# Making the first head pair's q and k by token blocks inside the first normalization, with most of V between the first pair's attention steps

## The reference

```
h = layernorm(x)
q, k, v = h @ Wq + bq, h @ Wk + bk, h @ Wv + bv      # 16 heads of 64
q, k = rope(q), rope(k)
attended = softmax(causal(q k^T / 8)) v
x = x + attended @ Wo + bo
g = layernorm(x)
xq = fp4(g);  wq = fp4(weights)                      # blocks of 16, max/6 scale, E2M1 grid
x = x + fp4(silu(xq @ wg^T) * (xq @ wu^T)) @ wd^T    # hidden width 2816
```

## Time and profile before

| what | us |
|---|---|
| median of 3 runs | 1466.71 |
| lowest, highest | 1452.48, 1481.68 |
| the profiled execution | 1454.53 |
| its longest span (core 3) | 1453.0 |
| spans of all cores | 1430.1 to 1453.0 |
| busy on core 3: PE, DVE, ACT | 1128.6, 1053.6, 785.0 |

### The profile page before, as it was taken

One profiled execution on the slowest core, in us unless ns is written; L12 is line 12 of the kernel. 1 busy time (PEld: TensorE's weight loads), 2 busy tenths in 40 slices (PEclk: granted clock), 3 DMA queues, 4 the chain that ended last, 5 costly groups with the idle time before them and its releaser, 6 DMA issues.

```text
span 1453.0 us, 18420 instructions; the slowest of 8 cores (1430.1 to 1453.0 us)
## 1 busy us (share of the span) xinstructions
PE 1128.6 (78%) x6112; PEld 466.1 (32%) x6112; DVE 1053.6 (73%) x1189; ACT 785.0 (54%) x1116; POOL 98.3 (7%) x195
## 2 busy tenths in 40 slices
PE   1996878778878787871595627999999999999997
PEld 0332222222222222220131213444444444444443
DVE  3453799978898979882731237888888888888885
ACT  2553868767777778882641344444444444444443
POOL 1001001010101010120111100000000000000000
PEclk9998999988889999995797958999999999999999
DMA  9624658595859695679587530000000000000000
GB/s 209 161 78 97 130 125 182 137 160 121 195 126 180 121 174 133 156 154 264 108 214 270 161 112 1 30 30 30 30 30 30 29 30 29 30 30 30 15 15 30
DMA packets 110636, 152.01 MB, mean 105 GB/s; under 512 B 76288, under 2 KB 77776, under 8 KB 107728
## 3 DMA queue, kind: packets, MB, share of 16 engines
q1 hardware_dynamic: 96112, 103.31, 29.2%
q0 software_dynamic: 14432, 47.54, 14.3%
HBM read 102.38 MB, written 32.11 MB: 93 GB/s over the span
## 4 chain that ended last, share of the span: by engine, by line
DVE 30%; PE 28%; DMA 19%; issue 14%; ACT 6%; POOL 2%; SPq 1%; DVEq 1%; ACTq 0%; POOLq 0%
PE ps L1048 13%; DMA rb<-rscr 5%; DMA xscr<-x_t 5%; PE ps L513 4%; PE ps L1088 4%; DVE qs_bm L275 3%; DVE sm_bm L275 3%; DVE qy L305 3%; DVE qx L300 3%; PE ps L571 3%; DMA rscr<-rn 2%; DMA sw<-qk 2%; DMA bqks<-bqk 2%; DMA qx<-wd 2%; DVE h_u L1075 2%
## 5 line engine op out<-in xcount | busy, mean ns | idle before, releaser
L705 ACT ACTIVATE PT<-ps,nb 128x1024 bf16<-128x1024 f32 (+1 forms) x320 | 301.0, 986 | 24.5 <-PE ps L693 13.3
L686 PE MATMUL ps<-qk 64*128 64x512 bf16 (+3 forms) x640 | 125.1, 383 | 145.8 <-ACT PT L705 124.9
L1048 PE MATMUL ps<-wgT,xqT 128*128 128x512 bf16 (+1 forms) x768 | 193.0, 400 | 5.3 <-ACT xqT L1022 5.3
L293 ACT ACTIVATE sm_nsh<-sm_bmc 128x64 f32<-128x64 f32 (+1 forms) x64 | 16.2, 253 | 314.7 <-DVE h_u L290 287.4
L1048 PE MATMUL ps<-wuT,xqT 128*128 128x512 bf16 (+1 forms) x768 | 175.2, 372 | 0.0
L1088 PE MATMUL ps<-wdT,hqT 128*128 128x512 bf16 x704 | 161.3, 382 | 5.8 <-ACT hqT L1022 5.8
L571 PE MATMUL ps<-xlT,wqk 128*128 128x512 bf16 x512 | 134.5, 413 | 20.2 <-ACT PT L705 17.3
L725 PE MATMUL ps<-PT,V 128*64 128x512 bf16 (+3 forms) x640 | 128.1, 397 | 0.4
L686 PEld LDWEIGHTS ps<-qk 64*128 64x128 bf16 x640 | 35.6, 94 | 284.3 <-issue 283.5
L725 PE MATMUL ps<-PT,ones 128*64 128x512 bf16 (+3 forms) x640 | 121.5, 377 | 0.0
L1048 PEld LDWEIGHTS ps<-wgT,xqT 128*128 128x128 bf16 x768 | 79.5, 106 | 90.2 <-issue 32.2
(11 more groups left out here) (97 smaller groups left out, 1556.4 us busy)
## 6 DMA issues: line engine op xcount, KB each, us to landing
qx<-wg SPq DMA_DIRECT2D x22, 512.0 KB, 4.5
qx<-wu SPq DMA_DIRECT2D x22, 512.0 KB, 4.3
x_a<-x SPq DMA_DIRECT2D x16, 512.0 KB, 6.8
sw<-qk POOLq DMA_DIRECT2D x64, 128.0 KB, 3.7
qx<-wd SPq DMA_DIRECT2D x16, 512.0 KB, 4.4
x_t<-x POOLq DMA_DIRECT2D x16, 512.0 KB, 4.8
out<-x_t SPq DMA_DIRECT2D x16, 512.0 KB, 2.6
rb<-rscr POOLq DMA_DIRECT2D x14, 512.0 KB, 9.2
```

The source lines that it names most:

```text
L686: ins = te.matmul(PS[k].ap()[:, 512 * h + o:512 * h + 512], q[r, 1, kc * 128:(kc + 1) * 128], q[r, 0, qb * 512 + o:(qb + 1) * 512], start= ...
L705: exp_a[n] = act((lambda c: c.activation(PT[j].ap()[:, :, o:512], sc[:, :, o:512], AFT.Exp, bias=nb12.ap(), scale=0.125)), [(sPE, pp)] + ( ...
L1048: ins = te.matmul(bank[:, 0:cn], xqT[t % 2].ap()[:, kc, :], w.ap()[:, n0:n1, kc, :], start=(kc == 0), stop=(kc == KC - 1))
```

## The change

Block b of the normalization no longer makes V. After each second block, 512 tokens are complete: q and k of pair 0 for them are made at once (`qk_half(0, which, b // 2)`), swapped (`swap_first`), and rotated in the next block (`rope_first`, three DVE operations over q and k of 512 tokens, with the tables broadcast). Three pieces of weight jobs go into a block instead of two; the twelve pieces that stood around the old q and k of pair 0 are gone, and four stand around V of tiles 0 to 3, which comes after the loop. V of tiles 4 to 15 is made and copied out at steps 0, 2, 3, 4, 6, 8, ... 20 of pair 0. Pair 0 takes 1.6/8.6 of the remaining weight jobs. `norm_recip` moves from step 5 to 8 and `norm_mult` from 14 to 24 (19 in the last pair); the last pair's own move too. The first loads are ordered anew: the q and k bias by SP, V's weights on POOL behind the first q and k weights and the rotation tables.

```
@@ loads
-        for j in range(4):
-            wv_ld = dma("gpsimd", sWV, ...)
-        dma("gpsimd", sCST, bvs[:], bv_h)
-        dma("gpsimd", sCST, bos[:], bo_h)
-        cst = dma("gpsimd", sCST, bqk[:], bqk_h)
+        bqk_ld = dma("sync", sBQ, bqk[:], bqk_h)
...
         load_wqk(0)
         dma("gpsimd", sTAB, cosb[:], cos_h)
         tab = dma("gpsimd", sTAB, sinb[:], sin_h)
+        dma("gpsimd", sCST, bvs[:], bv_h)
+        cst = dma("gpsimd", sCST, bos[:], bo_h)
+        for j in range(4):
+            wv_ld = dma("gpsimd", sWV, ...)
         load_wqk(1)
@@ qk_half
-            pp = pe(f, [(sWQ[p % 2], wq_ld[p]), (sACT, evac_done),
+            pp = pe(f, [(sWQ[p % 2], wq_ld[p]), (sACT, a_evac[4 * tb + 3]),
@@ new
+        def swap_first(tb):
+            sl = slice(tb * 512, (tb + 1) * 512)
+            for g in range(4):
+                o, i = 32 * g, 32 * (g ^ 1)
+                sw_d[0, tb] = dma("gpsimd", sSZ[tb], sw.ap()[o:o + 32, :, sl],
+                                  raw[0].ap()[i:i + 32, :, sl],
+                                  [(sACT, qk_a[0, 1])])
+
+        def rope_first(tb):
+            sl = slice(tb * 512, (tb + 1) * 512)
+            q = raw[0].ap()[:, :, sl]
+            s = sw.ap()[:, :, sl]
+
+            def bc(table):
+                return table.ap()[:, sl].unsqueeze(1).broadcast_to(
+                    [128, 2, 512])
+            dve((lambda v: v.tensor_tensor(q, q, bc(cosb), Alu.mult)),
+                [(sSZ[tb], sw_d[0, tb]), (sTAB, tab)])
+            v2 = dve((lambda v: v.tensor_tensor(s, s, bc(sinb), Alu.mult)),
+                     [])
+            rope_tb[tb] = dve((lambda v: v.tensor_tensor(
+                q, q, s, Alu.add)), [(sDVE, v2)])
@@ loop over b
             vn = ln1_negm(b, a)
-            pump(1)
+            pump(2)
             for t in (t0, t0 + 1):
                 ln1_apply(t, vn)
                 if t + 4 < NT:
                     load_xa(t + 4)
-            if b >= 1:
-                v_evac(t0 - 2)
-                v_evac(t0 - 1)
             for t in (t0, t0 + 1):
                 ln1_transpose(t)
                 ln1_evac(t)
-            for t in (t0, t0 + 1):
-                v_proj(t)
-        v_evac(NT - 2)
-        v_evac(NT - 1)
+            if b % 2 == 1:
+                for which in range(2):
+                    qk_half(0, which, b // 2)
+                swap_first(b // 2)
+            elif b:
+                rope_first(b // 2 - 1)
+        for t in range(4):
+            v_proj(t)
+            if t >= 1:
+                v_evac(t - 1)
+            pump(1)
+        v_evac(3)
+        rope_first(3)
@@ scores
-            pp = pe(f, [(sDVE, rope_v[p, 0]), (sDVE, rope_v[p, 1]),
-                        (sACT, sc_free[k])])
+            ws = ([(sDVE, rope_tb[qb])] if p == 0 else
+                  [(sDVE, rope_v[p, 0]), (sDVE, rope_v[p, 1])])
+            pp = pe(f, ws + [(sACT, sc_free[k])])
@@ whole_pair
-            share = (QTOT - q0) / (NP - p)
+            share = (QTOT - q0) * (1.6 / 8.6 if p == 0 else 1 / (NP - p))
...
+                if p == 0 and s in V_AT:
+                    v_proj(V_AT[s])
+                    v_evac(V_AT[s])
...
-                if prev_tok and s == 5:
+                if prev_tok and s == 8:
                     norm_recip(prev_tok[0])
-                if prev_tok and s == 14:
+                if prev_tok and s == (24 if p + 1 < NP else 19):
                     norm_mult(prev_tok.pop(0))
@@ last_pair
-            for qb, at_r, at_m in ((0, 16, 20), (1, 22, 28), (2, 34, 38)):
+            for qb, at_r, at_m in ((0, 20, 28), (1, 22, 32), (2, 30, 38)):
@@ before the pairs
-        for which in range(2):
-            for tb in range(4):
-                qk_half(0, which, tb)
-                pump(1)
-            swap(0, which)
-        for which in range(2):
-            pump(2)
-            rope(0, which)
```

More of the change, by code:

```diff
@@ L126, in build_nc @@
     sCST = mksem("sCST")
+    sBQ = mksem("sBQ")
+    sSZ = mksems("sSZ", 4)
     sTAB = mksem("sTAB")
@@ L404, in build_nc @@
             idn_ld = dma("gpsimd", sIDN, t[:], src)
-        for j in range(4):
-            wv_ld = dma("gpsimd", sWV, wv.ap()[:, 2 * j:2 * j + 2, :],
-                        wv_h[:, j * 2048:(j + 1) * 2048]
-                        .rearrange("p (c n) -> p c n", c=2))
-        dma("gpsimd", sCST, bvs[:], bv_h)
-        dma("gpsimd", sCST, bos[:], bo_h)
-        cst = dma("gpsimd", sCST, bqk[:], bqk_h)
+        bqk_ld = dma("sync", sBQ, bqk[:], bqk_h)
         wq_ld = {}
@@ L420, in build_nc @@
         tab = dma("gpsimd", sTAB, sinb[:], sin_h)
+        dma("gpsimd", sCST, bvs[:], bv_h)
+        cst = dma("gpsimd", sCST, bos[:], bo_h)
+        for j in range(4):
+            wv_ld = dma("gpsimd", sWV, wv.ap()[:, 2 * j:2 * j + 2, :],
+                        wv_h[:, j * 2048:(j + 1) * 2048]
+                        .rearrange("p (c n) -> p c n", c=2))
         load_wqk(1)
@@ L527, in v_evac @@
             sc_free[k] = a_v[t]
[L529 to L534, removed]
-            for t in (t0, t0 + 1):
-                v2 = ln1_stats(t)
-            a = ln1_rstd(b, v2)
-            pump(1)
-            vn = ln1_negm(b, a)
-            pump(1)
[L541 to L544, removed]
-            if b >= 1:
-                v_evac(t0 - 2)
-                v_evac(t0 - 1)
[L548 to L551, removed]
-                v_proj(t)
-        v_evac(NT - 2)
-        v_evac(NT - 1)
-        evac_done = a_evac[NT - 1]
         qk_a = {}
@@ L584, in qk_half @@
                 scale=1.0)),
-                [(sPE, pp), (sCST, cst)]
+                [(sPE, pp), (sBQ, bqk_ld)]
                 + ([(sPE, s_last[p - 2])] if p >= 2 else []))
@@ L607, in rope @@
                 q, q, s, Alu.add)), [(sDVE, v2)])
+        def swap_first(tb):
[18 more added lines that the diff above has]
+                q, q, s, Alu.add)), [(sDVE, v2)])
+        rope_tb = {}
+        for t in range(4):
+            load_xa(t)
+        for i in range(3):
+            w_load(i)
+        for b in range(NT // 2):
+            t0 = 2 * b
+            for t in (t0, t0 + 1):
+                v2 = ln1_stats(t)
+            a = ln1_rstd(b, v2)
+            pump(1)
+            vn = ln1_negm(b, a)
+            pump(2)
+            for t in (t0, t0 + 1):
+                ln1_apply(t, vn)
+                if t + 4 < NT:
+                    load_xa(t + 4)
+            for t in (t0, t0 + 1):
+                ln1_transpose(t)
+                ln1_evac(t)
+            if b % 2 == 1:
[4 more added lines that the diff above has]
+                rope_first(b // 2 - 1)
+        for t in range(4):
+            v_proj(t)
+            if t >= 1:
+                v_evac(t - 1)
+            pump(1)
+        v_evac(3)
+        rope_first(3)
+        rope_v[0, 0] = rope_v[0, 1] = rope_tb[3]
         nrm = {"n": 0, "dn": {}, "ds": {}, "rb": {}, "recip": {}}
@@ L648, in norm_recip @@
             if i >= 1:
-                ws.append((sDVE, mult_v.get(i - 1, 0)))
+                ws.append((sDVE, mult_v.get(min(i - 1, NP - 2), 0)))
             for h in range(2):
@@ L669, in build_nc @@
         HALF = {1 + 4 * n: (n // 4, n % 4) for n in range(8)}
+        V_AT = {0: 4, 2: 5, 3: 6, 4: 7, 6: 8, 8: 9, 10: 10, 12: 11, 14: 12,
+                16: 13, 18: 14, 20: 15}
         n_step = [0]
```

## The result

The changed kernel takes 1493.5 us in the median (1492.2 to 1504.4, 4 runs), the kernel before 1462.8 beside it: ratio 1.0231, 95% interval 1.015 to 1.031. A second measurement, beside the experiments, gave 1.0250 (1.021 to 1.029). It is slower, by 34 to 36 us of some 1455. (Ratios compare undisturbed runs only.)

What follows compares the result with a forecast made beforehand. It took V's matmuls on PE to bound the normalization, and PE and ACT in mid-pair, DVE from about step 20, the pairs. Terms -3 + 60 - 31 - 9 = +17 on the profiled 1454.5 gave 1471.5; forecast 1475, range 1440 to 1508.

Steps and rivals of the forecast that it cites:

- The likeliest case: Whole kernel: pair 0 about 60 us longer and half of it won back; chance 0.55.
- the prediction's own sign of being wrong: Wrong if pair 0's steps 21 to 39 take under 38 us, or normalization blocks overlap that were counted one after another.
- all that it wanted to see: Among others: PE over 95% busy to step 20 of pair 0, DVE over 90% after, pairs 1 to 4 of 63 to 67.
- Normalization: Before the pairs: DVE, ACT and PE follow one another, two blocks take 27.0 us, first scores at 142: -3 us.
- my one slow and one fast half: Odd normalization block: the two `qk_half` cost 3.5 and 1.9 us, the first meeting a low clock.
- Pair 0, steps 0 to 20: V adds 51.6 us of PE to 29.4, with only 4.4 idle to fill: 81 us in place of 33.8.
- DVE's sum was its time, I scale: Pair 0, steps 21 to 39: DVE's work grows from 33.1 to 45.8 us, so the stretch goes from 33.5 to 46.
- The share's -16: Pairs 1 to 6: 3.8 less DVE work per pair and the multiplication moved: 2.6 to 3.1 us in each, -16.
- The second gain: Pairs 1 to 6: of 22.1 us of DVE waits for `rb`, -15 us is won by ten more steps.
- the slow rival: Pairs: swap behind the later broadcast load on POOL's queue delays the rotation; +21 with half the pairs slow: 1492; chance 0.2.
- Pair 7: Last pair: starving by weight loads stays, 3.8 of DVE goes, block scales get 4 steps more: -9 us, bounds -3 and -14.
- The fast rival: Pair 0's late jobs slip beside V, it ends at PE's sum, +38: total -5, 1449.5 to 1461; chance 0.25.

Runs made afterwards that it cites:

- the runs with V back in: Changed kernel with each block making its V, bias load last, even share: 1.0018; also with the earlier kernel's scaling steps: 0.9981, both to the kernel before.
- the even share: Changed kernel with pair 0's share of the weight jobs back to an eighth: ratio 1.0353 to the kernel before.
- the three fastest runs: V in blocks, earlier scaling, q and k a block later: 0.9854; plus multiplication at 19: 0.9821; plus a fourth weight-job piece per block: 0.9810, to the kernel before.

## Why the prediction was right, and where its terms were off

The sign and the range (1440 to 1508) held; the size did not. The sum gave +17, the measured difference is +34 to +37, twice as much, and the time given, 1475, is 18.5 under the 1493.5 measured. The likeliest case was the right one: pair 0 grows by more (+54) than the pairs behind it win back (-24). But the prediction's own sign of being wrong came true, steps 21 to 39 under 38 us (34.5), and so did not all that it wanted to see: PE is 91% busy to step 20 and not 95%, and pair 1 takes 73.9 us and not 63 to 67. Its terms:

**Normalization, +7.2 for -3.** The mechanism, one block behind the other, was right, and the terms of the chain were too small. Two blocks took 30.9 us on core 2 for my 27.0: the rotation comes 8.7 us after the copies and not 6.0 (1.9 of issue and 4 of landing), which is 2.7 of the 3.9, and q and k take 6.42, 1.0 more than my 5.4. On other cores and in other blocks q and k take 5.07 to 6.50; so my one slow and one fast half is the lower end, and two slow ones would be 7.0 by the row's 3.5. The Trainium skill (TensorE: Matmul & The Clock Gate, section Loop structure matters more than you think) would have both halves slow; this trace agrees with the low clock (granted 0.56 in the 6.5 us of q and k) and lies between the two prices. The first mean also waits for a tile that lands 4.4 us later, the small bias load ahead of it on SP; I had it "as before" and "the reordered first loads cost nothing". How much of the start that is stays open, since the start hardly moved when the load went last. That the blocks are not slow for want of V is shown by the runs with V back in; that they are for the place of q and k and its rotation, by the run with both a block later.

**Pair 0, steps 0 to 20, +52.6 for +47.** V at PE's price (12 x 4.3 = 51.6) was right. I let it fill the 4.4 us of idle time; it filled none. Beside V at the attention's pace PE stands 87 us for 79 busy.

**Pair 0, steps 21 to 39, +1.4 for +13.** Here the step "DVE's sum was its time, I scale" failed. DVE's sum had matched the stretch before because DVE came into it with work left over from the steps ahead. With V there DVE is clear at step 21, and the even share shows what is left: 27.1 us with DVE busy 21.8. The larger share adds 7.5, and pair 1 takes 73.9 us in place of 67.4 and, with the even share, 67.8: work of pair 0 on DVE slides into it. Pair 0's total, 121.4, lies in the forecast 120 to 132 because the misses of its two parts, +5 and -12, partly cancel.

**Pairs 1 to 6, -13.5 for -31.** The share's -16 was right as a sum (402.7 and 403.2 against 418.9 with the even share), but by luck: I had 2.6 to 3.1 in each of six pairs, and pair 1 lost 6 while the five others won 22. The second gain, -15 for the waits for `rb`, did not come: a DVE that no longer waits at step 14 is early at step 20 and waits for the swap. I had that wait as the slow rival, but made it hang on the broadcast just ahead on the queue. With the reciprocal back at 5 the wait drops by a fifth to three tenths only (to 18.2 from 22.6 and 25.6), so the broadcast is the smaller part; that DVE arrives before the swap has landed is the larger, as the wait of 3.2 us shows where the multiplication stands right ahead of the rotation. This rival held in its place and its size per core, not in its cause, and that its total, 1492 on the profiled execution, is so near the 1492.2 measured is luck: +10 in the normalization and +5 and -12 in pair 0 nearly cancel beside it.

**Pair 7, -10.3 for -9**, of which the share is 5 (84.4 against 89.3) and the scaling steps of the last pair 4 to 5 (91.0 against 94.7 alone, 88.9 against 93.6 with V in the blocks).

**The fast rival** (late jobs slip beside V, pair 0 at +38) was half true: the late part is short, but the early part grew by all of V.

Open: what delays the landing of the first tile by 4.4 us when an 8 KB load stands ahead, and what that costs the start; what else than the broadcast makes the swap late; why the waits for transposes grow when others go; whether the multiplication at step 19 wins anything; and the parts of the last 0.4% between the three fastest runs.

## What to carry to other kernels

Work moved out of a loop that it seemed to bind only helps if what is left is shorter than that work; draw the chain from one turn to the next through each engine's queue first, and put the consumer of a turn's result one turn later, behind the next turn's start. Filler between the steps of a loop that is bound by two engines costs its full price on the busy one, and hides work of a third. A wait removed on an in-order engine is worth only the distance to the next wait on it: list the arrivals that follow before counting the gain, and where two transfers are awaited, put the work that needs the earlier one right ahead of the one that needs the later (here that removed most of both waits, for a ratio of 0.996). Before a busy sum is taken for a stretch's time, ask whether it holds work left over from the stretch before. And measure the same kernel twice before a stage's few us are explained.

## What the runs showed of the hardware

- With a load of 8 KB ahead of the 512 KB loads on SP's queue the fifth of these landed at 22.5 to 25.4 us on all eight cores of five profiles; with that load behind them, the one edit, at 19.0 to 21.3. The delay is about the 4.3 to 4.7 us from one landing of these loads to the next in the kernel before (core 3), though the small load carries 1/64 of the bytes.
- The 16 matmuls of q and k, of 512 columns each, took 5.07 to 6.50 us in the changed kernel, where PE idled before the transposes ahead of them (on core 2 by 6.2 us for the first 16, which took 5.38, and by 15.4 for the second, which took 6.42); 3.61 to 6.57 with V in the same blocks, where PE waited 2.1 to 3.4 us right before them; and 3.62 or 3.63 each time with q and k a block later, where PE had no idle time before them. The 6.42 us, at a granted clock of 0.56:

```profile
71.60:78.10 6.50, 6.42 (x16) 2.19 (x16) 0.00 (x0) 0.69 (x1) 0.00 (x0) 0.56 0.21 55
```

- A DVE operation on two bf16 tensors, one of them a table repeated over an outer dimension, took 0.69 us for 1024 columns, a little over half of the 1.23 for 2048 without repetition. The Trainium skill (VectorE: DVE Perf Modes, section What auto-detection actually checks) asks for 16-bit tensors of step 1, and the trace agrees.
